# Last downs, weight passes and gathered rows at the seam between an expert feed-forward and an attention, moved

## The reference, cut to what matters

```python
x = x + _L0_attn_ref(_layernorm(x), ...)                 # 16 heads of 16
x = x + _L0_xattn_ref(ctx, ctx, _layernorm(x), ...)      # long convolution
x = x + _L0_ffn_ref(_layernorm(x), ...)                  # 8 experts, top 1, and a shared expert
x = x + _L1_attn_ref(_layernorm(x), ...)                 # attention 1
x = x + _L1_xattn_ref(_layernorm(x), ctx, mask)          # memory attention
x = x + _L1_ffn_ref(_layernorm(x), ...)                  # feed-forward on ternary weights

def _L0_ffn_ref(h, router_w, w1, v1, w2, shared_gate, shared_up, shared_down):
    ...
    for e in range(E):                                   # the routed expert of each token
        out = out + dense_w[:, e:e + 1] * _glu(x, w1[e], v1[e], w2[e])
    return out + _glu(x, shared_gate.T, shared_up.T, shared_down.T)   # the shared expert
```

## Time and profile before

| | us |
|---|---|
| runs: 676.9, 677.09, 684.29; median | 677.09 |
| the profiled execution, its own time | 678.24 |
| its span, from the first to the last instruction | 676.5 |
| TensorE busy in the span | 598.0 |
| VectorE busy | 521.5 |
| ScalarE busy | 394.4 |
| GpSimd busy | 324.6 |

### The profile page before, as it was taken

The page is one execution under the profiler, slowest core; times in us unless marked ns, Lnnn a source line. Parts: engine busy times, 40 slices in busy tenths (PEclk is TensorE's granted clock), DMA queues, the critical chain, the costliest instruction groups (busy, mean ns, idle before and its releaser), DMA issues.

```text
span 676.5 us, 15765 instructions
## 1 busy us (share of the span) xinstructions
PE 598.0 (88%) x4624; PEld 459.1 (68%) x4626; DVE 521.5 (77%) x1189; ACT 394.4 (58%) x826; POOL 324.6 (48%) x632
## 2 busy tenths in 40 slices
PE   6999999998999799999998689999998777649786
PEld 5788888875655565588886578888887533237565
DVE  5788999984999977353226689999999578699995
ACT  2677777773333133263331467777777367878993
POOL 1243555534998441233313634433333568486882
PEclk9999999999999999999999789999999699968999
DMA  8401000010346861523334200000000000000011
GB/s 288 156 3 35 2 0 0 0 33 12 62 67 195 326 237 35 172 71 90 83 71 139 63 26 9 2 2 0 0 0 1 1 1 1 0 0 2 0 63 63
DMA packets 23779, 39.13 MB, mean 58 GB/s; under 512 B 2864, under 2 KB 20032, under 8 KB 22576
## 3 DMA queue, kind: packets, MB, share of 16 engines
q1 hardware_dynamic: 21760, 33.31, 15.4%
q0 software_dynamic: 1968, 5.16, 3.0%
HBM read 31.22 MB, written 7.24 MB: 57 GB/s over the span
## 4 chain that ended last, share of the span: by engine, by line
PE 58%; DVE 16%; issue 14%; POOL 5%; ACT 2%; DMA 2%; DVEq 2%; SPq 0%; POOLq 0%; ACTq 0%
PE ps L801 6%; PE ps L334 6%; PE ps L1288 6%; PE ps L362 4%; PE ps L372 4%; PE ps L321 4%; PE ps L1156 4%; PE ps L382 3%; PE ps L344 3%; PE ps L1298 3%; DVE work L576 3%; DVE work L582 2%; DVE wide L1970 2%; PE ps L1215 2%; PE ps L399 2%
## 5 line engine op out<-in xcount | busy, mean ns | idle before, releaser
L497 ACT COPY wide<-ps 128x512 f32<-128x512 f32 x126 | 74.5, 593 | 43.2 <-PE ps L334 41.1
L229 POOL TENSOR_TENSOR var_eps<-mv,powers 128x1 f32<-128x1 f32 x80 | 16.7, 208 | 157.0 <-DVE mv L220 156.9
L576 DVE TENSOR_REDUCE work<-ps 128x8 f32<-128x1024 f32 x64 | 77.9, 1218 | 12.4 <-PE ps L321 12.3
L492 ACT ACTIVATE work<-work 128x1024 f32<-128x1024 f32 x64 | 68.4, 1069 | 20.2 <-DVE work L582 19.9
L334 PE MATMUL ps<-ident,work 128*128 128x128 f32 x512 | 75.8, 280 | 3.2 <-DVE work L605 1.2
L582 DVE TENSOR_TENSOR work<-ps,work 128x1024 f32<-128x1024 f32 x64 | 77.9, 1217 | 0.6
L334 PEld LDWEIGHTS ps<-ident,work 128*128 128x128 f32 x512 | 58.7, 143 | 19.2 <-issue 13.2
L1923 PE MATMUL ps<-w_o,wide 128*128 128x128 f32 x256 | 35.6, 297 | 25.6 <-DVE w_o L1962 12.7
L1334 POOL DMA_INDIRECT work<-tokens,small x23 | 23.4, 1018 | 63.3 <-PE ps L1263 45.9
L1923 PEld LDWEIGHTS ps<-w_o,wide 128*128 128x128 f32 x256 | 33.2, 210 | 29.3 <-DVE wide L1952 15.5
L362 PE MATMUL ps<-xnT,w_qkv 128*128 128x128 f32 x256 | 38.4, 296 | 12.5 <-DVE work L582 9.8
(11 more groups left out here) (233 smaller groups left out, 1531.9 us busy)
## 6 DMA issues: line engine op xcount, KB each, us to landing
wide<-in_expert_gu SPq DMA_DIRECT2D x1, 4096.0 KB, 14.1
sorted_y<-work SPq DMA_DIRECT2D x23, 128.0 KB, 1.7
xn_all<-in_ctx_rev_t SPq DMA_DIRECT2D x1, 2048.0 KB, 10.4
small<-hank SPq DMA_DIRECT2D x16, 128.0 KB, 3.8
w_qkv<-hank SPq DMA_DIRECT2D x16, 128.0 KB, 3.8
wide<-in_expert_d SPq DMA_DIRECT2D x1, 2048.0 KB, 9.2
ctx_sb<-in_ctx SPq DMA_DIRECT2D x1, 2048.0 KB, 8.4
ctxT<-in_ctx_t SPq DMA_DIRECT2D x1, 2048.0 KB, 13.0
```

The costliest lines, as they stand in the source:

```text
L492: act.activation(prob2[g], prob2[g], ACT.Exp, scale=ATT_SCALE).then_inc(s["exp"], 1)
L497: act.copy(probT[r], turned(t, r)).then_inc(s["pT"], 1)
L576: dve.tensor_reduce(mxs[:, 8 * g:8 * g + 8], S2[g], AX.X, ALU.max).then_inc(s["mx"], 1)
```

## The change

Eight edits, all around the seam. (1) VectorE runs the two weight passes ahead of down 2 and ahead of down 3. (2) The last three downs on VectorE: 5 between statistics and normalization of tile 0, 6 in the same place of tile 1, 7 in the body of tile 1. (3) TensorE makes only downs 2 to 6 behind the slots and down 7 in attention 1's body 0, behind the transposes of tile 1; downs 6 and 7 get other banks, and the waits of TensorE for VectorE's adds between them go. (4) What follows the experts on TensorE and ScalarE waits for six adds instead of eight. (5) The five unread multiplications ahead of attention 1 go. (6) GpSimd fetches the third group (tiles 2 and 3) between the square roots of tiles 0 and 1. (7) In attention 1 the memsets stand behind the normalization of tile 0 and the keys of tile 0; ScalarE waits for each apart. (8) The load of the feed-forward's row vectors waits for the values of attention 1's tile 5 (the count is 16 of attention 0 and 6).

```diff
...
@@ pe_early_1
                     front_transpose(pe, f, t + 1, 1 - u, X)
+                if isinstance(t, int):
+                    beside("pe amid", pe, t)
                 follow("pe", pe, t, u, 0, X=X[:, D:2 * D], KO=M)
@@ tensor (attention)
                 before(pe, "pe")
-                if layer == 1:
-                    keep_busy(pe, T[0], ident, 5)
                 front_transpose(pe, f, 0, 0, X)
@@ scalar (attention)
+                act.wait_ge(s["ones"], 2 * layer + 1)
+                act_v(act, 0, 0)
                 act.wait_ge(s["ones"], 2 * layer + 2)
-                act_v(act, 0, 0)
@@ vector (attention)
                     beside("dve amid", dve, t - 2)
-                    dve.memset(va[t], 1.0).then_inc(s["ones"], 1)
+                    if layer == 0:
+                        dve.memset(va[t], 1.0).then_inc(s["ones"], 1)
                     front_xn(dve, f, t, t)
+                    if layer == 1 and t == 0:
+                        dve.memset(va[0], 1.0).then_inc(s["ones"], 1)
                     beside("dve", dve, t - 2)
                 dve.wait_ge(cols_loaded, 32)
                 dve_keys(dve, 0, 0)
+                if layer == 1:
+                    dve.memset(va[1], 1.0).then_inc(s["ones"], 1)
                 beside("dve rows", dve, -1)
@@ gpsimd (attention)
                 front_rstd(pool, f, 0, 0)
+                beside("pool amid", pool, -1)
                 front_rstd(pool, f, 1, 1)
@@ experts
-            DOWN_BANK = [0, 1, 2, 3, 0, 1, 2, 3]
+            DOWN_BANK = [0, 1, 2, 3, 0, 1, 4, 6]
@@ pe_shared
-                    if q >= 4:
-                        pe.wait_ge(s["x_shared"], q - 3)
@@ gpsimd (experts)
-                for n in range(3):
-                    pool_gather(pool, n)
+                pool_gather(pool, 0)
+                pool_gather(pool, 1)
@@ tensor (experts)
-                pe_shared(pe, DOWN_FIRST, NB // 2)
+                pe_shared(pe, DOWN_FIRST, NB // 2 - 1)
@@ vector (experts)
-                for q in range(DOWN_FIRST, NB // 2 - 2):
-                    dve_down(dve, q)
                 beside_slots("dve", dve, "later")
+                dve_down(dve, 2)
                 beside_slots("dve", dve, "later end")
+                dve_down(dve, 3)
+                dve_down(dve, 4)
                 dve_gathered(dve, 0, 1)
@@ beside (experts)
-                if name == "dve amid" and t == -2:
-                    dve_down(eng, NB // 2 - 2)
-                    dve_down(eng, NB // 2 - 1)
+                if name == "pool amid":
+                    pool_gather(eng, 2)
+                if name == "pe amid" and t == 0:
+                    pe_shared(eng, NB // 2 - 1, NB // 2)
+                if name == "dve amid":
+                    dve_down(eng, t + 7)
                 if name == "dve" and t == -2:
                     dve_gathered(eng, 1, 2)
+                if name == "dve rows" and t == 1:
+                    dve_down(eng, NB // 2 - 1)
@@ slots_done
-                    eng.wait_ge(s["x_shared"], NB // 2)
+                    eng.wait_ge(s["x_shared"], 6)
@@ sync (feed_forward)
                 sp.wait_ge(s["w_done"], 2)
+                sp.wait_ge(att_sem["v_ps"], NB + 6)
                 sp.dma_start(rows, a["ffn_rows"].partition_broadcast(P)).then_inc(s["rows_loaded"], 16)
...
```

## The result

The changed kernel takes 669.77 us (median of 3 runs, 669.26 to 671.31) against 677.09: a ratio of 0.987, 95% interval 0.983 to 0.991. The forecast was 671.0, its range 667.8 to 675.0. Its profiled execution took 671.31 us with a span of 669.5, against 676.5.

A forecast was written before the change was run, and what follows sets the result against it. VectorE's order was taken to bound the seam between expert feed-forward and attention 1, while VectorE idles inside it. Terms −5.05 − 1.69 + 0.65 = −6.09 us, counted from the median 677.09, gave 671.0; range 667.8 to 675.0.

The forecast's parts named there:

- Order at the seam, −5.05: Between expert feed-forward and attention 1: VectorE's new order and the dropped fillers start the first transpose at 365.45 instead of 370.50, −5.05 us.
- the landing of row 0: Tile 0's gathered row, fetch issued at 359.75: taken to land at 362.2, the trace bounding it by 362.2 and 366.67.
- Both passes fall into waits for TensorE and cost nothing: VectorE's two weight passes between downs: hidden while VectorE waits for TensorE, cost 0; without that cover 2.48 us.
- Fillers, "1.2 us of it": Five unread multiplications ahead of attention 1: 1.2 us of the −5.05 us come from removing them.
- Row vectors, taken as 0: Later load of the feed-forward's row vectors: between −0.5 and 0 us, taken as 0, no row showing anything waiting.
- holds in tile 0's lull, −1.69: TensorE's wait behind tile 1's transposes: down 7 splits it, the clock stays up for tile 1, −1.69 us.
- The second fall: Clock fall in attention 1's tile 1 (0.66 at 390 to 395): left unchanged, with down 7 on VectorE charged +0.65 us there.
- second rival: Clock holds in tile 1 too: scores 1 to scores 2 in 9.0 to 9.5 us, total 668.6 to 669.1; chance 0.12.
- a pause of 2.26 us: TensorE's standstill at the seam before the change, clock still 1.00; taken as evidence that shorter waits keep the clock.
- The cold seam: Rival: without fillers the clock falls ahead of tile 0's queries, gain only −0.7 us, total 676.4; chance 0.03.
- late and cold: Rival: row 0 lands just ahead of 366.67 and TensorE's clock falls at the seam, +3.35 us, 680.4; chance 0.04.
- gain taken back: Rival: second gather delays tile 1's square root or later rows, attention loses 5 us again, 676 to 677; chance 0.04.

## Why the prediction was right, and where its steps were off

**Order at the seam, −5.05: right in kind, 0.65 too much.** Passes between the downs, down 5 inside the square root, transposes right behind the normalization: all as replayed. The failing step is the landing of row 0, taken as 2.45 us behind the fetch's issue from the traffic rows of before; it was 3.30. VectorE waited 0.48 us for it, the bulk of the shortfall. "Both passes fall into waits for TensorE and cost nothing" overlooked GpSimd: the second pass runs from 362.44 to 363.66, over the start of the first fetch, and that fetch is 0.52 us longer. Over the fourteen profiles this holds without exception: in eight the second pass overlaps the first fetch and it takes 1.46 or 1.47 us; in six it does not, and it takes 0.94 or 0.95. One of the six has the changed kernel's own order at the seam, the run with more fillers at the start, in which the late store brought the fetch in behind the pass:

```profile
358.93 1.22 DVE L1722 TENSOR_SCALAR xnT_all<-xn_all 128x2048 bf16<-128x2048 f32 x1
361.03 0.95 POOL L1359 DMA_INDIRECT wide<-sorted_y,small  x1 [16.95 <-DMA sorted_y<-work]
```

There the fetch landed 2.58 us behind its start instead of 3.30. Of the order's parts, the passes are shown (1.9 us), and down 7 ahead of the transposes (0.8 to 0.9); that downs 6 and 7 and the memset no longer stand ahead of tile 0's normalization was not run by itself.

The Trainium skill (DMA: Bandwidth & Descriptors, SWDGE vs HWDGE vs iDMA) says that GpSimd writes its transfers' descriptors into memory from which VectorE locks it out while VectorE runs in a two-port mode. The trace agrees in direction; which mode the pass ran in no row names.

**Fillers, "1.2 us of it": wrong as a share, without harm to the sum.** Alone they are worth 0.5 us at the first transposes, because memset and normalization stood right behind them. The 5.05 had been worked out from the whole new order, not added up from shares.

**Row vectors, taken as 0 ("no row shows anything waiting for those"): mis-sized.** This was true of the old order, and the runs agree (the wait alone: 0). In the new order the load would have been issued beside the fetch of row 0; without the wait the kernel loses 5.8 us, and the seam 8.1. I replayed the new order on four engines and not on SyncE's queue, where the same replay would have put the load at about 361. The sum came out right only because the new order and the wait were both in it.

**Clock.** The step "holds in tile 0's lull, −1.69" came true as a mechanism: without the down in the lull the clock falls (4.15 against 5.09 us and more, above). Its size did not: from tile 1's first query to its scores pass 4.16 us instead of 5.44, −1.28. From the first transposes to scores 1 13.22 us pass instead of 15.43, −2.21; the other 0.93 lies ahead of that query, where the prediction had no term. VectorE takes the maximum of tile 0 2.53 us behind the start of the first scores in the kernel before:

```profile
377.66 1.23 DVE L576 TENSOR_REDUCE work<-ps 128x8 f32<-128x1024 f32 x1 [2.30 <-PE ps L321]
```

And 1.58 us behind it in the changed kernel:

```profile
375.60 1.22 DVE L577 TENSOR_REDUCE work<-ps 128x8 f32<-128x1024 f32 x1 [0.96 <-PE ps L321]
```

This distance is 2.53 to 2.55 in three of the profiles with the old order (before, the passes alone, the wait alone) and 1.20 to 1.77 in the other eleven, with and without the down in the lull; what makes it stays open. At scores 1 the forecast of some 6.7 us earlier met 6.61 by luck: the seam gave 0.65 less and tile 0 0.52 more.

The second fall, "left where it is" with +0.65 for down 7, went as well: scores 1 to scores 2 −1.85 net, 9.54 us, next to the 9.0 to 9.5 of the second rival. So the seam gave −4.40 − 2.21 − 1.85 = −8.46, and that rival, with a chance of 0.12, described it better than the forecast did. Which edit kept the clock in tile 1 stays open: from scores 1 to scores 2 the fourteen profiles do not separate by any one edit (9.5 to 12.6 us with the down in the lull, 9.5 to 14.1 without).

The measure by which the prediction argued, a pause of 2.26 us that left the clock at 1.00, did not hold in every execution: behind it and the fillers the clock stayed at 1.00 in the profiles of before, of the wait alone and of the passes alone (2.86 us there), but not in the repeat of the kernel before. There the fillers and tile 0's queries were:

```profile
369.35 1.52 PE L71 MATMUL ps<-ident 128*128 128x128 f32 x10 [2.25 <-issue]
...
371.96 2.04 PE L362 MATMUL ps<-xnT,w_qkv 128*128 128x128 f32 x8 [0.66 <-issue]
```

The mean granted clock from 370 to 375 is 0.54 there, that is 1.2 GHz for most of it. So that the clock held at the seam and in the lull followed less surely than the prediction had it.

The Trainium skill's rule weighed in the prediction (TensorE: Matmul & The Clock Gate, What's actually happening: the throttled state is the default) did not bite at the seam: TensorE waited 0.77 us there, and the clock stayed 1.00 with and without fillers. The cold seam did occur where the wait was longer, 4.85 us with the load early, 3.00 with only the fillers gone, 2.59 with the passes back, 1.22 with the third group of fetches back; it did not behind 1.68 us with more fillers at the start.

**What made 8.45 into 7.0.** Tile 0 of attention 0 took the times of half clock in the profile of the changed kernel. TensorE's first queries in the kernel before:

```profile
7.16 1.16 PE L362 MATMUL ps<-xnT,w_qkv 128*128 128x128 f32 x8 [0.98 <-DMA w_qkv<-in_w_qkv]
```

And in the changed kernel:

```profile
7.56 2.07 PE L362 MATMUL ps<-xnT,w_qkv 128*128 128x128 f32 x8 [1.23 <-DMA w_qkv<-in_w_qkv]
```

That is 350 us ahead of the first edited instruction. Kernels that differ only at the seam start in either way or between (scores 0 of attention 0 at 10.64 us with the load early, 13.92 with only the fillers gone), yet each kernel profiled twice repeated its own start within 0.1 us. What decides it was not found; that the new program as a whole has a hand in it can't be excluded. The −1.81 behind tile 3 goes with the clock in the later stages (a mean of 0.94 from there to the end before, 0.96 after), and most of it is gone in the repeat of the kernel before, which took 268.74 us there. The forecast's nearness to the median thus owes something to chance: a seam worth 2.4 us more than the sum, and a start that cost 3.3.

**Right without remark:** GpSimd's fetches between the square roots held up tile 1's normalization (0.77 us) without touching the path; the later tiles kept 8.94 us; the rivals "late and cold" and "gain taken back" did not occur, though the kernel without the load's wait shows the mechanism of the first: a late row, 4.85 us of waiting, half clock.

## What to carry to other kernels

When an engine's order changes, replay every queue that its semaphores release, the transfers too: an edit that costs nothing in the old order can decide the new one, and an edit that is worth nothing alone (the load's wait, 0 on the old kernel) can carry most of the gain beside the others (5.8 us in the changed one). Work that has to be done somewhere can be placed inside a lull in which TensorE's clock falls without it. Compare marks inside the stage that was changed, not only spans: here the ends of the span moved by 3.3 and 1.8 us for reasons that lie outside that stage.

## What was not expected of the hardware

A GpSimd fetch that started inside a VectorE pass over on-chip memory took 1.46 us instead of 0.94. A load of 1.5 MB on SyncE's queue delayed a fetch issued 0.67 us before it from 3.3 to 7.4 us. At the start of the program the granted clock in the rows reads 1.00 while TensorE's instructions take 2.07 us instead of 1.16, so the durations look like a low clock that the clock rows don't show. And with the clock at 1.00 in it, tile 1 took 9.54 us from scores to scores in the changed kernel, 10.3 with fillers at either place and 10.99 with the passes back; the surplus stands between a transpose (L334) and ScalarE's copy of it, and stays unexplained.
